# A graph network's edge loop: second bias and relu of the first way on VectorE, two SBUF operations on GpSimd

## The reference

```python
def _mlp(x, w1, b1, w2, b2, w3, b3):
    x = jax.nn.relu(x @ w1.T + b1)
    x = jax.nn.relu(x @ w2.T + b2)
    return x @ w3.T + b3

def _prop_once(node_states, f_idx, t_idx, edge_features, w1, ...):
    edge_inputs = jnp.concatenate([node_states[f_idx], node_states[t_idx], edge_features], axis=1)
    edge_states = _mlp(edge_inputs, w1, b1, w2, b2, w3, b3)
    return jax.ops.segment_sum(edge_states, t_idx, num_segments=node_states.shape[0])

agg = _prop_once(x, src, dst, edge_attr) + _prop_once(x, dst, src, edge_attr)
```

## Time and profile before

| | us |
|---|---|
| timed runs, median of 3 | 2269.78 |
| lowest and highest of them | 2264.28, 2269.97 |
| the profiled execution | 2273.58 |
| its span, first to last instruction | 2271.8 |

### The profile page before, as it was taken

The page is one execution under the profiler, slowest core; times in us unless marked ns, Lnnn a source line. Parts: engine busy times, 40 slices in busy tenths (PEclk is TensorE's granted clock), DMA queues, the critical chain, the costliest instruction groups (busy, mean ns, idle before and its releaser), DMA issues.

```text
span 2271.8 us, 39842 instructions
## 1 busy us (share of the span) xinstructions
PE 2211.9 (97%) x13211; PEld 1846.2 (81%) x13211; DVE 1779.6 (78%) x4139; ACT 1165.7 (51%) x2015; POOL 1166.0 (51%) x858
## 2 busy tenths in 40 slices
PE   4999999999999999999999999999999999899997
PEld 3888888888888888888888888888888864577776
DVE  7888898898889889889889988898988836603212
ACT  4555556556556555565555555655655533311112
POOL 2466666666666666666666666666656630001100
PEclk9999999999999999999999999999999999999999
DMA  4356454455445455445444544554544367196965
GB/s 154 68 116 146 92 114 96 90 116 103 90 102 108 91 104 114 92 92 115 94 101 111 98 90 104 105 100 97 113 92 91 58 110 256 63 366 259 383 265 194
DMA packets 242852, 292.67 MB, mean 129 GB/s; under 512 B 126804, under 2 KB 200359, under 8 KB 234688
## 3 DMA queue, kind: packets, MB, share of 16 engines
q1 hardware_dynamic: 168498, 236.63, 33.3%
q0 software_dynamic: 73216, 54.58, 18.7%
q10 hardware_dynamic: 1040, 0.52, 0.1%
HBM read 218.56 MB, written 73.08 MB: 128 GB/s over the span
## 4 chain that ended last, share of the span: by engine, by line
PE 93%; DMA 3%; DVE 2%; issue 1%; POOL 0%; ACT 0%; SPq 0%; DVEq 0%; POOLq 0%; ACTq 0%
PE bank L1270 19%; PE bank L1333 13%; PE bank L1283 13%; PE bank L1293 8%; PE bank L1361 8%; PE bank L2216 8%; PE bank L1345 4%; PE bank L1366 4%; PE bank L1231 4%; DMA l_ring<-adj 3%; PE bank L1329 2%; PE bank L1881 2%; PE bank L1310 2%; PE bank L1889 1%; PE bank L1311 1%; PE bank L2230 1%
## 5 line engine op out<-in xcount | busy, mean ns | idle before, releaser
L514 POOL DMA_INDIRECT sums<-outb,target x416 | 662.4, 1592 | 551.6 <-ACT outb L698 440.5
L507 POOL DMA_INDIRECT xg<-in_x,gidx x416 | 477.4, 1148 | 150.3 <-issue 142.6
L653 ACT ACTIVATE h1h<-hpre 128x512 fp32r<-128x512 f32 x416 | 258.0, 629 | 131.0 <-DVE hpre L898 94.0
L902 DVE SCALAR_TENSOR_TENSOR h1l<-hpre,h1h 128x512 fp32r<-128x512 f32 x416 | 268.5, 687 | 17.1 <-ACT h1h L653 11.9
L898 DVE TENSOR_TENSOR hpre<-pb,bank 128x512 f32<-128x512 f32 x416 | 265.6, 679 | 4.7 <-ACT pb L648 3.9
L1270 PE MATMUL bank<-sdh,w1h 128*128 128x512 f32 x624 | 246.9, 396 | 3.4 <-DVE sdl L930 2.7
L1270 PE MATMUL bank<-sdh,w1l 128*128 128x512 f32 x624 | 247.8, 397 | 0.0
L1270 PE MATMUL bank<-sdl,w1h 128*128 128x512 f32 x624 | 245.0, 393 | 0.0
L1333 PE MATMUL bank<-w2h,h1l 128*128 128x256 f32 x832 | 234.0, 281 | 0.0
L1333 PE MATMUL bank<-w2l,h1h 128*128 128x256 f32 x832 | 233.6, 281 | 0.0
L1333 PE MATMUL bank<-w2h,h1h 128*128 128x256 f32 x832 | 233.5, 281 | 0.0
(11 more groups left out here) (282 smaller groups left out, 4706.2 us busy)
## 6 DMA issues: line engine op xcount, KB each, us to landing
l_ring<-adj SPq DMA_DIRECT2D x54, 1568.0 KB, 8.3
rowb<-along SPq DMA_DIRECT2D x104, 512.0 KB
ef<-in_edge_attr SPq DMA_DIRECT2D x103, 256.0 KB
adj<-band SPq DMA_DIRECT2D x46, 480.0 KB
adj<-band SPq DMA_DIRECT2D x23, 540.0 KB
stay<-adj SPq DMA_DIRECT2D x6, 1568.0 KB, 14.8
xg<-in_x,gidx POOLq DMA_INDIRECT x416
sums<-outb,target POOLq DMA_INDIRECT x416
```

The source lines that it names most:

```text
L507: pool.indirect_dma_start(out=to, out_offset=None, in_=a["x"], in_offset=bass.IndirectOffsetOnAxis(ap=ids, axis=0)).then_inc(s_x[par], 16)
L514: pool.indirect_dma_start(out=tables[k % 2], out_offset=bass.IndirectOffsetOnAxis(ap=target[par][:, 1, k:k + 1], axis=0), in_=outb[par][:, ...
L653: nc.scalar.activation(h1h[:, way, f, :], hpre[:, f, way, :], ACT.Relu).then_inc(s_h1, 1)
L902: nc.vector.scalar_tensor_tensor(out=h1l[:, f, way, :], in0=hpre[:, f, way, :], scalar=0.0, in1=h1h[:, way, f, :].bitcast(fp32), op0=ALU.m ...
```

## The change

- **The bias of the first way's second layer** is no longer added by a matmul. relu(z + b) = max(z, -b) + b. ScalarE negates the bias row once (`b2row`), and VectorE takes max(z, -b) from the bank into `he` (`upright`, in VectorE's `turn` once after `places` and once after `count_pairs`). The + b is constant for each edge, so it is added to b3 once, through the third layer's weights, at the end of the loop (two matmuls of one row and a one-row add). ScalarE's `upright` and TensorE's L1329 are gone.
- **GpSimd** gets `match` and one of the four lower parts (f = 1, way 1) in a function `extra`, which stands in its queue after the gathers of a turn. GpSimd's subtraction has no max, so ScalarE first takes the relu of that `hpre` tile in place, between the last `h1h` and `es`. VectorE does three `rest`, with (1, 0) ahead of (0, 1), and TensorE waits for the last two lower parts only before the second way.
- **VectorE's order**: `nodes` waits for the sum before last, not the last one, and may so run ahead of it; `compare` waits for the last one. The two registers of `count_pairs` are loaded together, after the first `upright` and ahead of `sums`.

```diff
@@ pool, windowed
+                def extra(g, par):
+
+                    pool.wait_ge(s_cmp, g + 1)
+                    if not (isinstance(g, int) and g == 0):
+                        pool.wait_ge(s_cs, g * 2 - 1)
+                    nc.gpsimd.tensor_tensor(match[:, :, :], same[par][:, :, :],
+                                            lower[:, :].unsqueeze(1).broadcast_to([P, K, P]), ALU.mult).then_inc(s_match, 1)
+                    pool.wait_ge(s_h1x, g + 1)
+                    nc.gpsimd.tensor_tensor(h1l[:, 1, 1, :], hpre[:, 1, 1, :], h1h[:, 1, 1, :].bitcast(fp32),
+                                            ALU.subtract).then_inc(s_h1p, 1)
...
+                    if ahead:
+                        extra(j + 1, 1 - par)
@@ scalar
                     hidden(1, 1)
+                    if win:
+                        nc.scalar.activation(hpre[:, 1, 1, :], hpre[:, 1, 1, :], ACT.Relu).then_inc(s_h1x, 1)
...
-                    if win:
-                        upright(g, 0)
-                    else:
+                    if not win:
                         second(g, 0)
@@ vector, ways
                 both(1)
+                rest(1, 0)
                 rest(0, 1)
-                rest(1, 0)
-                rest(1, 1)
+                if all_four:
+                    rest(1, 1)
@@ vector, windowed
                     if not early:
-                        dve.wait_ge(s_sum, (g - 1) * 2)
+                        dve.wait_ge(s_sum, (g - 1) * 2 - 1)
...
+                def upright(g, n):
+
+                    if isinstance(g, int) and g == 0:
+                        dve.wait_ge(s_b2, 1)
+                    else:
+                        dve.wait_ge(s_sum, g * 2 - 1)
+                    dve.wait_ge(s_l2, g * 4 + (n + 1))
+                    nc.vector.tensor_tensor(he[:, 2 * n:2 * n + 2, :], bank[6 + n][:, :].rearrange("p (t u) -> p t u", t=2),
+                                            b2row[:, :].unsqueeze(1).broadcast_to([P, 2, H]), ALU.max).then_inc(s_he, 1)
...
                     places(g, par, early=early > 0)
+                    upright(g, 0)
+                    slots = slots_of(g)
                     if ahead:
                         sums(g + 1)
...
-                    count_pairs(g, 0)
-                    count_pairs(g, 1)
+                    for half in range(2):
+                        count_pairs(g, half, slots[half])
+                    if not begin:
+                        upright(g, 1)
@@ tensor, windowed
                     if n == 0:
-                        pe.wait_ge(s_h1l, g * 4 + 4)
+                        pe.wait_ge(s_h1l, g * 3 + 2)
...
-                    nc.tensor.matmul(bank[6 + n][:, :], ones_r[:, :], b2hl[:, :, :].rearrange("p t u -> p (t u)"),
-                                     start=True, stop=False)
...
+                    pe.wait_ge(s_h1l, g * 3 + 3)
+                    pe.wait_ge(s_h1p, g + 1)
                     for n in range(2, 4):
                         pe.wait_ge(s_he, g * 2 + (n - 1))
                         second(g, n)
```

72 lines of the change are left out of this document (33 added, 39 removed).

## The result

| | before | after |
|---|---|---|
| median of 4 runs, us | 2268.16 | 2416.07 |
| lowest to highest, us | 2264.28 to 2269.97 | 2398.76 to 2419.53 |
| profiled execution, us (its span) | 2273.6 (2271.8) | 2415.0 (2413.3) |
| ratio, 95% interval | | 1.0629 [1.0608, 1.0649] |

The changed kernel is 148 us slower. The forecast was 2388 us, with a range up to 2410. The sign was right, and so was the mechanism that was forecast. The time is 28 us above the forecast and 6 us above the range. From the first point 0 of the edge loop to the last, 103 turns, it took 1763.7 us before and 1905.6 now. That is 141.9 us more; the two profiled executions differ by 141.4, so nothing outside the loop matters.

The account below looks back on a forecast made before the run. TensorE bounds now; afterwards the ring over VectorE, ScalarE and `es`. That ring plus GpSimd's clash gives 18.3 us a turn, 1.15 more, 120 us over 104 turns: 2273.6 + 120 less 3.8 is 2390, said 2388; range 2258 to 2410.

Parts of the forecast that it names:

- point 0: Start of a turn of the edge loop: the end of the last `total` matmul of the turn before.
- TensorE's saving: Two bias matmuls fewer a turn, 0.23 us each: 0.46 us a turn, 48 us if TensorE alone set the pace.
- From `es` to point 0: End of ScalarE's `es` to the end of TensorE's last eight matmuls: 1.35 us, read from one turn.
- the slack: Room on the path VectorE, ScalarE, `es` before it delays TensorE: 0.38 us a turn.
- A ring without a clash: Loop point 0, VectorE, ScalarE, `es`, point 0, with engines not disturbing each other: 17.54 us a turn, 41 us longer in all.
- That VectorE stands still under GpSimd: VectorE operations with two SBUF operands stop for the whole of a GpSimd operation; the forecast case, chance 0.45.
- Where the clash lands: At the turn's end: `match` 15.0 to 16.3, two `h1l` to 17.6, GpSimd's `h1l` to 18.9 stopping `into`.
- P + c = 19.25: Turn length P plus lateness c of `same` at the turn's start; gave c = 0.86 and P = 18.4 us.
- The second bias-and-relu: On VectorE in front of `sdl`, ending at 6.51 us; TensorE wants its bank at about 6.5, wait 0.1 us at most.
- GpSimd's own time costs nothing: GpSimd's two new operations, 2.1 to 2.6 us, fit its 4.06 us idle between last gather and next scatter.
- case 1: The forecast itself, VectorE standing still under GpSimd: 2377 to 2402 us, chance 0.45.
- rival 5: GpSimd's operations last longer under VectorE's traffic and push its scatters: over 2410 us, chance 0.06.

Follow-up runs that it names:

- e3: The kernel before, plus a ScalarE relu in place on `hpre` between the last `h1h` and `es`: 2279.11 us, 1.0054.
- e1: The changed kernel with GpSimd's two new operations shrunk to two columns each, ScalarE's relu writing the fourth lower part: 2301.25 us, 1.0137.
- e2: As e1, with both of VectorE's register loads moved to the end of the turn before: 2252.73 us, 0.9923.
- e5: The changed kernel, with GpSimd's `match` also waiting for ScalarE's relu, so both GpSimd operations stand behind it: 2375.18 us, 1.0456.
- e6: The changed kernel with `match` and the fourth lower part back on VectorE, no new GpSimd work, no relu in place: 2357.59 us, 1.0386.
- e7: As e6, with both register loads moved to the end of the turn before: 2270.32 us, 1.0018.
- e4: The kernel before, plus four spare GpSimd operations of 128x256 a turn, two after the last gather, two after the fourth `h1h`: 2389.12 us, 1.0542.
- e8: As e4, at the same places, but with eight GpSimd memsets of 128x256 instead of the four operations that read: 2451.83 us, 1.0795.
- e9: As e4, but with all four spare GpSimd operations in front of the scatters: 2438.17 us, 1.0752.

## What of the prediction held, and which step failed

- **TensorE's saving** of 0.46 us a turn is real and unused, as said: TensorE does not set the pace.
- **The relu in front of `es`**: forecast 0.55 us, measured 0.51 (e3). Right.
- **The two loads**: forecast 0.48 us between bare and hidden, measured 0.47 (e1 against e2). Right. `sd` at 3.1 was forecast, 3.18 measured; `hpre` 11.17 against 11.27.
- **From `es` to point 0**: forecast 1.35, measured 1.21. The step "P = 16.19 + 1.35" is mis-sized by 0.14, and with it the slack, 0.51 in place of 0.38. One turn stood for all, and part of its 0.40 us in front of the eight matmuls was not `es`. A ring without a clash is 17.45 us, not 17.54: 2301 us, not 2310.
- **"From `sdl` to `hpre` nothing changes: 4.75 us"** held in e1, but in e5 and in the usual turn of e6 it was 4.44. This made these turns shorter than the forecast's steps have them.
- **That VectorE stands still under GpSimd** was taken at its full price, from the far row `l_wz`, and it is so: the `h1l` of 1.85 us above. The Trainium skill's rule, in "SBUF — State Buffer", section "Who interferes with whom", agrees with these traces here: two SBUF inputs are stopped, one input or a bank is not, and GpSimd's writes alone stop nobody. On who goes first they differ, see the end.
- **Where the clash lands** is the step that failed. "VectorE then has two `h1l` left ... they run from 16.35 to 17.6" and "P + c = 19.25" assumed that `match` is over before the last two `h1l`, that they then run free, that only `into` is stopped, and that each turn is like the last, with one c for all. Only the long turns end like this, and there `match` has already stopped the first `h1l`, and `same` starts 0.1 us late. In the turns of 17.9 us both `h1l` are stopped and `into` is not. That their `same` starts 0.86 us late, which is the forecast c, is therefore luck, and with it the turn comes out at 17.88 and not 18.40: 0.14 less behind `es`, 0.31 less from `sdl` to `hpre`, and 0.07 because `same` starts at 0.11 and not at 0.04 even without a clash. With these turns alone the kernel would have been faster than forecast. What made it slower is that turns differ. In the short turns GpSimd's second operation falls on the same `h1l` as its first, so another `h1l` and `into` are still to be done, and `same` is 1.76 us late. And a late VectorE meets a GpSimd that is on time, so in the next turn `match` hits the first `h1l`, in front of `hpre`. The 27 turns of 20 us and more bring the mean to 18.50.
- **How the loss divides.** By the loops of the three traces it is 30 us from the kernel before to e1 (the ring over `es`), 71 more to e5 (a clash at the turn's end), and 41 more to the changed kernel; they add up to the 142 us found. e5 also moves the clash from the `h1l` to `same`, so the 41 us are not `match` in front of `hpre` alone. Read directly, the second pair of `hpre` stands later than in e1 by 26 us in sum, in 23 of 90 turns; the turns with half clock have some 8 us more; the rest is not divided.
- **The second bias-and-relu** was priced at 0.1 us at most: "TensorE wants that bank ... at about 6.5. It ends at 6.51". In e1 it ends at 6.59 and TensorE's wait is nothing in the median. But a late `same` makes it late by the same amount, and the forecast, with c = 0.86, did not carry c to this place. TensorE waits for it in 78 turns of the changed kernel, 75.6 us. At the medians this ring is 0.2 us shorter than the one over `es`, so there it adds nothing. In e6 and e7 it sets the turn.
- **GpSimd's own time costs nothing** held here: GpSimd still waits for `outb` before its next scatter (1.85 us at 1321.50 in the turn of 17.9 us), and it has 0% of the chain. As a general sentence it was too bold (e4, e8, e9).

The range went wrong with the same step. Its top was called the top of case 1, though case 1 ends at 2402, and nothing in it stood for turns of unequal length. The time lies where rival 5 has it (over 2410, chance 0.06), but not by rival 5's mechanism: GpSimd's two operations have means of 1284 and 1341 ns against the 1.27 us of the earlier trace rows, and no scatter is pushed.

Of the signs named: TensorE's idle time before the last eight matmuls, released by `es`, is there (39.1 us in 47 turns); so are the long `h1l` and `into`, `hpre` later than 11 us, `es` 0.52 us after the relu (1017.51, 1018.03), and the second `sd` more than 1.2 us after the relu. A turn of 18.1 to 18.5 is right for the mean (18.50) and for about one single turn in nine.

Left open: whether GpSimd's `match` in front of the scatters, 1.3 us where 2.3 are free by the estimate above, would win something. That wasn't run.

## What to carry to other kernels

Before work goes from VectorE to GpSimd, write beside each GpSimd operation which VectorE operations run under it, and count all those with two SBUF operands as stopped for its whole length: that can be more than what VectorE gives away. Do this over two turns and with the first one late, since a clash that makes VectorE late changes what the next one hits. Measure the tail behind a near-critical step where the consumer really waits for it, not in a turn that only looks late. And when a turn comes out as forecast, check that the wait you forecast is the one that ends last: in e6 the number was right and the path another.

## What the runs showed of the hardware

- A GpSimd operation that reads SBUF stops a VectorE operation with two SBUF operands, sometimes also one whose record has begun. The `h1l` at 1017.04 started 0.36 us before `match`, lasted through both GpSimd operations, and ended 0.56 us after them (at 1020.46), nearly a whole operation's time. The length of the head start does not decide. Beside a `match` that follows directly on a gather's issue, an `h1l` that had started 0.69 us earlier was stopped too (3.74 us, at 1167.71). Where GpSimd's operation came after a wait for ScalarE, an `h1l` with a head start of 0.55 us (30 times in the changed kernel) or 0.63 us (all through e5) kept its 0.68. The Trainium skill's section named above gives the right of way to the one that issues first. By the records alone the first case is against it and the second for it; GpSimd's spans are rough by the profile's own account, and what a record's start means for the ports, no run here shows.
- GpSimd can be held up in turn. Its `h1l` took 1.27 us in the short turns, 1.38 in the turn of 17.9 us, and 1.47 in e5, where `into` ran until 980.61, after GpSimd's record had begun at 980.29.
- Small operations are stopped as well. Four elements a partition took 0.56 us in place of 0.16 (e9).
- GpSimd's memsets stop nothing: `match` 683 ns beside them, 684 without (e8).
- Gathered rows could be used 1.6 us after the end of the gather's issue on GpSimd (median of 78 waits in e9).
- Two register loads in a row on VectorE, behind a 0.69 us operation, left 0.67 us of idle time in front of `sd` (1024.65). Where VectorE waits anyway they cost nothing that shows. Moved by a few lines they are worth 49 us of this kernel (e1 against e2), and 0.59 us a turn where the second bias-and-relu sets the pace (e6 against e7, 87 us between the medians, with e6's stretches at half clock in it).
- TensorE's granted clock fell to half for 3.4 us at a time, seldom 6.8, eight times in the changed kernel's loop and 27 times in e8's, after waits of TensorE that were mostly 1.4 us and longer. In e5, with a wait of 1.08 us in each turn, it never did.
